# Four graph layers on one core: table blocks of five instead of six, a multiplication moved to GpSimd, and a reordered last pair pass

## What is computed

```python
def _L1_gnn_ref(z, P, W1, b1, W2, b2, Wu, bu):      # "maximum"
    m1z = z @ W1.T + b1
    m2z = z @ W2.T + b2
    pair = relu(m1z[:, :, None, :] + m2z[:, None, :, :])
    mask = (swapaxes(P, 1, 2) != 0)[..., None]
    m = max(where(mask, pair, -inf), axis=2)
    return relu(concatenate((z, m), axis=-1) @ Wu.T + bu)

def _L2_gnn_ref(input, adj, W, a_w, a_b):           # "heads", H = 8
    h = input @ W
    ...
    att = softmax(where(adj[:, None] > 0, e, NEG_INF), axis=-1)
    return einsum('bhij,bjf->bif', att, h) / att.shape[1]

def _L3_gnn_ref(x, A_init, ...):                    # "pairs"
    D = abs(x[:, :, None, :] - x[:, None, :, :])
    h = D @ W1.T + b1            # statistics over all pairs of all graphs
    h = leaky((h - m) / sqrt(v + EPS) * g1 + be1)
    s = where(A_init > 0, h @ W2.T + b2, NEG)
    y = softmax(s) @ x @ Wg.T + bg   # statistics over all nodes of all graphs
    y = leaky((y - mg) / sqrt(vg + EPS) * gg + beg)
    return concatenate([x, y], axis=2) @ Wt.T + bt
```

## Time and profile before

| | us |
|---|---|
| median of 3 runs (2192.54 to 2194.11) | 2193.01 |
| the profiled execution | 2195.21 |
| its span, first to last instruction | 2193.4 |

### The profile page before, as it was taken

How to read it: one execution, slowest core, us unless ns; L and a number is a source line. 1 busy time by engine, 2 the same in 40 slices (tenths; PEclk the granted TensorE clock), 3 DMA queues, 4 the chain that set the end, 5 groups by cost and what they waited for, 6 DMA issues and landing times. The chain is left out here.

```text
span 2193.4 us, 43678 instructions
## 1 busy us (share of the span) xinstructions
PE 1839.7 (84%) x13419; PEld 1195.8 (55%) x13419; DVE 1829.3 (83%) x2792; ACT 1459.0 (67%) x3325; POOL 471.6 (22%) x346
## 2 busy tenths in 40 slices
PE   2978988888885888886799999999999577778786
PEld 1857777776772656565655555555555133333346
DVE  5988788888885999997799999999999466767666
ACT  0544444444443888885278888888888577777773
POOL 1510000000001111101444444444444100000001
PEclk9989999999996999997599999999999799999998
DMA  6000000000000000000045555555555889999972
GB/s 173 0 7 2 1 0 0 0 0 0 0 1 12 6 5 4 5 6 20 1 201 222 220 220 220 228 222 220 220 220 227 311 331 349 355 349 355 353 279 77
DMA packets 122544, 297.31 MB, mean 136 GB/s; under 512 B 20352, under 2 KB 56456, under 8 KB 122264
## 3 DMA queue, kind: packets, MB, share of 16 engines
q1 hardware_dynamic: 105336, 287.69, 35.0%
q10 hardware_dynamic: 16896, 8.39, 1.3%
q0 software_dynamic: 256, 0.56, 0.1%
HBM read 154.78 MB, written 141.82 MB: 135 GB/s over the span
## 5 line engine op out<-in xcount | busy, mean ns | idle before, releaser
L1234 POOL TENSOR_TENSOR v_pairs<-hd 128x2048 f32 (+1 forms) x64 | 269.4, 4209 | 310.8 <-DVE v_pairs L1259 310.8
L1319 ACT ACTIVATE v_hid<-v_psW 128x1024 f32<-128x1024 f32 x256 | 263.3, 1028 | 85.9 <-PE v_psW L1357 85.9
L1255 DVE TENSOR_TENSOR v_pairs<-v_psX,hd 128x2048 f32<-128x2048 f32 x128 | 292.3, 2287 | 17.5 <-PE v_psW L1357 17.5
L1357 PE MATMUL v_psW<-v_pairs,p_w1T 128*64 128x512 f32 x1024 | 288.8, 597 | 0.0
L724 DVE TENSOR_REDUCE m_part<-m_psS 128x128 f32<-128x1024 f32 (+1 forms) x192 | 216.9, 1130 | 68.6 <-PE m_psS L603 68.4
L1322 ACT ACTIVATE v_junk<-v_psW 128x1024 bf16<-128x1024 f32 x256 | 263.1, 1028 | 0.0
L1357 PE MATMUL v_psW<-v_pairs,l_w1T 128*64 128x512 f32 (+1 forms) x1024 | 252.5, 587 | 0.0
L603 PE MATMUL m_psS<-m_onehot,m_tableT 64*128 64x128 f32 x2816 | 217.3, 293 | 34.2 <-DVE m_part L724 18.0
L1348 PE MATMUL v_psW<-p_ends,v_weights 128*64 128x512 bf16 x1536 | 235.3, 381 | 4.3 <-DMA v_fold<-in_c_fold_dram 4.3
L956 ACT ACTIVATE a_ex<-a_eu,a_nmx 128x128 f32<-128x128 f32 x512 | 197.8, 389 | 37.3 <-PE a_psA L925 28.7
L603 PEld LDWEIGHTS m_psS<-m_onehot,m_tableT 64*128 64x128 f32 x2816 | 180.6, 194 | 59.3 <-ACT m_tableT L666 19.4
(11 more groups left out here) (253 smaller groups left out, 3539.6 us busy)
## 6 DMA issues: line engine op xcount, KB each, us to landing
pair_hidden<-v_hid SPq DMA_DIRECT2D x256, 512.0 KB, 2.6
s_h<-pair_hidden SPq DMA_DIRECT2D x128, 1024.0 KB, 7.3
s_wide<-pair_scores SPq DMA_DIRECT2D x64, 128.0 KB, 6.0
adj_ring<-in_adj_dram ACTq DMA_DIRECT2D x16, 256.0 KB, 6.2
x_all<-in_x_dram ACTq DMA_DIRECT2D x16, 256.0 KB, 6.0
out_dram<-o_res SPq DMA_DIRECT2D x16, 256.0 KB, 2.3
pair_scores<-s_rot SPq DMA_DIRECT2D x64, 32.0 KB, 6.0
p_ends<-in_c_ends_dram SPq DMA_DIRECT2D x1, 1024.0 KB, 4.8
```

The lines of the kernel that those rows point to most:

```text
L1234: nc.gpsimd.tensor_tensor(D[:, home(u, SLABS - 1), :].rearrange("c (h d i) -> c h d i", h=2, i=N), one, far, ALU.subtract).then_inc(psub_d ...
L1255: nc.vector.tensor_tensor(slab(s), own, windows(hd, n, s)[1], ALU.max).then_inc(max_done, 1)
L1319: nc.scalar.activation(hid[:, s, :], psW[:, buf, :], ACT.Identity, accum_out=hsum[:, bass.ds(m, 1)]).then_inc(evacuated, 1)
L1357: last = nc.tensor.matmul(psW[half * HID:half * HID + HID, buf, c:c + w], product[:, :], D[:, home(u, s), half * HALF + c:half * HALF + c ...
```

## The change

- **Blocks of five.** `BLK = 5`, `NBLK = 28`, `SUB = 32`, `NCH = 7` chunks of four blocks, `NG = 2` items of 4 and 3 chunks, `ITEMS = 8` a quad. Five table steps; the last one covers 16 blocks. `select` uses products of 32 rows; `q` runs over four and each `q` has a bank of `psS`, so that an item fills all four banks and waits for the reduction of the item before. `reduce` reads four banks; `merge` is one maximum of two tiles.
- **Order of the maximum.** PE and ACT prepare two items ahead (`select` first, `prepare(at + 2)` last in a slot). The update's bias and its `hT` half are done early (`own`, slot 5), the `mT` half in slot 2 of the next quad. The sum with the own term goes to a tile `both`, the bias instruction on DVE is gone. `prepare` of the table starts after DVE's first fill (`padded`).
- **Heads.** The multiplication with the reciprocal sums is done by POOL; `ex`, `zs` and `rz` have four buffers instead of two. POOL's normalization of quad g+2 follows in slot 1.
- **Pass 2.** The slabs of pass 1 and the load slots are one tile (`ring`); SP issues the first four loads at the end of pass 1. The read-back is two DMAs of 64 rows of 512 B; the first half lands in `fwd` itself, and two copies of 64x64 replace the addition. The features' part of the output product is done in pass 2 (`xo_mm`), where POOL adds the output bias to `x` and DVE adds the product.
- **Output.** Four products a quad instead of eight, one addition on DVE instead of two, no copy on POOL; the output DMA reads `k.x`.

```diff
-BLK = 6
-NBLK = (N + BLK - 1) // BLK
+BLK = 5
+NBLK = 28
-NCH = NBLK // 2
+NCH = NBLK // 4
...
-                    pe.wait_ge(reduced, done(n - 2))
-                    for c in range(4 * r, min(4 * r + 4, NCH)):
-                        for q in (0, 1):
+                    pe.wait_ge(reduced, done(n - 1))
+                    for c in chunks(r):
+                        for q in range(4):
                             rows = slice(SUB * q, SUB * q + SUB)
-                            last = nc.tensor.matmul(psS[:, 2 * par + q, b(c % 4)], tableT[rows, par, c % 4, :],
+                            last = nc.tensor.matmul(psS[:, q, b(c % 4)], tableT[rows, par, c % 4, :],
                                                     onehot[rows, par, c % 4, :], start=True, stop=True)
...
+                def own(g, p):
+                    pe.wait_ge(added, done(g - 1))
+                    nc.tensor.matmul(psU[:, :].rearrange("n (b c) -> n b c", c=C), one[:, :],
+                                     k.bu[0:1, :].unsqueeze(1).broadcast_to([1, G, C]), start=True, stop=False)
+                    for i in range(G):
+                        last = nc.tensor.matmul(psU[:, b(i)], hT[:, p, b(i)], k.wuT[:, 0, :], start=False, stop=False)
+                    last.then_inc(own_mm, 1)
...
                     for at in range(ITEMS):
...
+                        select(g, *divmod(at, NG))
+                        if at == 0 and next:
+                            turn(g + 1, 1 - p)
+                        if at == 1 and next:
+                            second(g + 1, 1 - p)
+                        if at == 2 and prev:
+                            update(g - 1, 1 - p)
+                        if at == 3 and next:
+                            first(g + 1, 1 - p)
+                        if at == 5:
+                            own(g, p)
+                        if at + 2 < ITEMS:
+                            prepare(g, *divmod(at + 2, NG))
...
-                    nc.vector.tensor_reduce(mx[:, b(i)], part[:, i, :, :].rearrange("z r i -> z i r"), AX.X,
-                                            ALU.max).then_inc(merged, 1)
+                    nc.vector.tensor_tensor(mx[:, b(i)], part[:, i % 2, 0, :], part[:, i % 2, 1, :], ALU.max).then_inc(merged, 1)
...
                     for at in range(ITEMS):
                         reduce(g, at)
                         if at == 0:
                             if prev:
                                 add_own(g - 1, 1 - p)
+                            tables(g, p, 2, LATE)
                         if at == 1:
+                            merge(g, 0)
+                            tables(g, p, 3, EARLY)
+                        if at == 2:
+                            tables(g, p, 3, LATE)
+                        if at == 3:
+                            merge(g, 1)
+                            if next:
+                                tables(g + 1, 1 - p, 0, EARLY)
+                        if at == 4:
+                            if prev:
+                                update(g - 1)
+                            if next:
+                                tables(g + 1, 1 - p, 0, LATE)
+                        if at == 5:
+                            merge(g, 2)
+                            if next:
+                                tables(g + 1, 1 - p, 1, EARLY)
+                            if prev:
+                                statistics(g - 1)
...
+                def slot(g, p, i, behind, ahead):
+                    n = g * G + i
+                    if behind(3):
+                        at = (i - 3) % G
+                        pool.wait_ge(recip, done(n - 3))
+                        per_head = ex[:, at, :].rearrange("n (h j) -> n h j", j=N)
+                        nc.gpsimd.tensor_tensor(per_head, per_head, rz[:, at, :].unsqueeze(2).broadcast_to([N, HEADS, N]),
+                                                ALU.mult).then_inc(scaled, 1)
+                    if i == 1 and ahead(2):
+                        normal(g + 2, p)
...
+                sp.wait_ge(w_mm, done(B * SLABS - 1))
+                for s in range(SLABS):
+                    sp.wait_ge(stored[s], 16 * B)
+                for j in range(4):
+                    load_products(sp, D, loaded, hidden, j)
...
                     sp.wait_ge(written[m % 2], 16 * (m // 2 + 1))
+                    sp.wait_ge(m_mm, done(m - 2))
+                    src = scratch[m % 4].rearrange("(i j) -> i j", j=2 * N)
+                    sp.dma_start(fwd[0:HID, m % 2, :], src[0:HID, 0:N]).then_inc(back[m % 2], 16)
                     sp.wait_ge(fwd_ready, done(m - 2))
-                    sp.dma_start(wide[:, m % 2, :], scratch[m % 4].rearrange("(i j) -> i j", j=2 * N)).then_inc(back[m % 2], 16)
...
+                    sp.dma_start(wide[HID:N, m % 2, :], src[HID:N, HID:HID + N]).then_inc(back[m % 2], 16)
...
-                        nc.vector.tensor_tensor(fwd[:, p, :], wide[:, p, 0:N], wide[:, p, N:2 * N], ALU.add).then_inc(fwd_ready, 1)
+                        nc.vector.tensor_copy(fwd[HID:N, p, 0:HID], wide[HID:N, p, HID:N])
+                        nc.vector.tensor_copy(fwd[HID:N, p, HID:N], wide[HID:N, p, 0:HID]).then_inc(fwd_ready, 1)
+                    if five:
+                        m = n - 5
+                        dve.wait_ge(xo_mm, done(m))
+                        dve.wait_ge(xb_ready, done(m))
+                        xs = k.x[:, bass.ds(m * C, C)]
+                        nc.vector.tensor_tensor(xs, psO[:, 0:C], xs, ALU.add).then_inc(x_added, 1)
...
                         pe.wait_ge(hg_ready, done(m - 1))
+                        pe.wait_ge(x_added, done(m - 1))
                         pe.wait_ge(hx_ready, done(m))
                         nc.tensor.matmul(psG[:, 0:C], hx[:, q, :], k.wgT[:, :], start=True, stop=True).then_inc(hg_mm, 1)
+                        nc.tensor.matmul(psO[:, 0:C], hx[:, q, :], k.wtT[:, 0, :], start=True, stop=True).then_inc(xo_mm, 1)
...
                     for i in range(G):
-                        nc.tensor.matmul(psU[:, p, b(i)], hq[:, p, b(i)], k.wtT[:, 0, :], start=True, stop=False)
-                        last = nc.tensor.matmul(psU[:, p, b(i)], yn[:, p, b(i)], k.wtT[:, 1, :], start=False, stop=True)
+                        last = nc.tensor.matmul(psU[:, p, b(i)], yn[:, p, b(i)], k.wtT[:, 1, :], start=True, stop=True)
```

More of the change, by code:

```diff
@@ L688, in _ @@
                 first(0, 0)
+                item(0, 0)
                 quads(act, quad)
@@ L757, in quad @@
                 def quad(g, p, prev, next):
-                    def ahead(i, steps):
-                        if next:
-                            tables(g + 1, 1 - p, i, steps)
                     for at in range(ITEMS):
                         reduce(g, at)
-                        if at % NG == NG - 1:
-                            merge(g, at // NG)
                         if at == 0:
@@ L1059, in phase_pairs @@
         hidden = nc.dram_tensor("pair_hidden", (B * SLABS, N, HALF), F32).ap()
+        ring = k.sb(ctx, "pair_ring", [N, SLABS + 1, SC], F32)
+        loaded = [k.sem(f"s_loaded{i}") for i in range(4)]
         with ExitStack() as hctx:
@@ L1685, in _ @@
             def _(dve):
-                for s in (leaky, biased, res_ready):
+                for s in (leaky, summed):
                     dve.sem_inc(s, BIAS)
```

249 lines of the change are left out of this document (107 added, 142 removed).

## The result

The changed kernel takes 2130.9 us (median of 4 runs, 2129.6 to 2132.9), the kernel before 2193.6 in the same comparison: a ratio of 0.9712, 95% interval 0.9695 to 0.9728. The profiled execution has a span of 2131.1 against 2193.4. So 63 us were gained where I had forecast 113; the sign was right, the size and the range were not.

The account below looks back on a forecast made before the run. Bounds: no full engine in the maximum, DVE in heads, a ring of ACT and PE in pass 2. Gains 63 (maximum) + 36 (heads) + 2 + 0 + 12 (output) = 113 from 2195.2: 2082.2, by the median 2080; range 2055 to 2122.

Parts of the forecast that it names:

- the picking's price: Maximum: rounds of four records on 32 rows; 32 records take 1.16 us and 24 take 0.94.
- C: Maximum: products on 32 rows run one after the other, 0.11 us a record; stage 190 longer, kernel 2333, chance 4%.
- the 2220 of the prediction: Maximum: if the skill's 81 ns a product held for the new products, slots of 2.7 and 2.1, kernel some 2220.
- I add 0.6 for clock dips and imperfect order: Maximum: 0.6 us added to a quad of 27.2, giving 27.8 against 31.86, a gain of 61 us.
- rival A: Maximum: PE becomes its bound, by record price or a clock staying at 1.2 GHz; no gain there, 2141, chance 12%.
- everything behind that wait on PE ... comes while DVE reduces, at most 2 us against 1.75 or more: Maximum: PE's turn, projections, own and prepare, at most 2 us, run during DVE's reduction of 1.75 us or more.
- the tail: End of the maximum: a gain of 2 us, as half the products and the bias are out of the way.
- rival B: Heads: DVE stays the bound because it and GpSimd block each other; 2109 us, chance 14%.
- Heads: the term: Heads: ACT bounds next, 4.6 us a graph instead of 5.18, a gain of 36 us for 63 graphs.
- Pass 2, the start and the output: Gains of 0 in pass 2, 2 us from pass 1 to pass 2, and 12 us in the output.
- D: Whole kernel: everything at its floor, gains of 72 + 43 + 5 + 15, 2058 us, chance 7%.
- E: Pass 2: a new wait, the `x` addition or read-back on the ring, 0.3 us a graph, 2100 us, chance 8%.

Follow-up runs that it names:

- m_all: Changed kernel with own part in three pieces, match products done four times, GpSimd's normalization held back until item 1 is picked: 2092.0 us, ratio 0.9534.
- h_att: Changed kernel with DVE's copy of the heads' attention moved from before its leaky part to after it: ratio 0.9628, 18 us less than the changed kernel.
- m_fill: Changed kernel with every match product of the maximum done four times over: ratio 0.9651, 13 us less than the changed kernel.

## Why the prediction was wrong

**Maximum, the picking's price: right.** 1.17 and 0.95 us for 1.16 and 0.94. The rival that they are dearer (C) is dead at 0.028 a record.

One sum beside it doesn't come out: with slots of 2.7 and 2.1 the time is about 2195, and the 2220 of the prediction follows only with 0.2 for two hand-overs added to each. Nothing rested on it.

**Maximum, "I add 0.6 for clock dips and imperfect order": the step that failed.** The mechanism stood in the text, that a PE with waits in every slot is granted a lower clock (rival A), and the term for its mild form was mis-sized. It measured 1.8 a quad against the forecast's slots: 1.0 in slot 5, where in ten of 14 inner quads the own part and the preparation ran slowed and the gap was 3.3 instead of 1.8, and 0.8 in slot 7, where in eleven of 14 the picking did (up to 2.09 us for 1.17). The mean clock hardly showed it, 0.90 instead of 0.94; the slow stretches lay on products that DVE waits for. The sum should have had a term for them, since the prediction itself counted about one dip a quad, showed what it costs, and the picking had just been put on the path in every slot. One picking of 32 records at 1.2 GHz is 0.9 us.

**Maximum, "everything behind that wait on PE ... comes while DVE reduces, at most 2 us against 1.75 or more": right at 2.4 GHz only.** In slot 5 PE is ready 2.33 us after its picking at full clock, 0.40 after the reduction's end, and DVE's other work hides this. At 1.2 GHz it is 3.2 to 3.9 us, and nothing hides it. I had seen that the two numbers hardly fit (2 against 1.75), and didn't ask what they are at the lower clock.

**Maximum, the tail: wrong sign.** I gave it a gain of 2, which the last update has (6.6 to 4.6 us), and did not look at the last quad. It lost 7.7. Of these 2.1 stay when the clock is up (25.1 in m_all against 23.0 before: the reductions are 2.5 longer), and 5.6 went with the clock of 0.72, while PE was busy 21 of 31 us. The forecast's form "a quad times 15, and 2" left the sixteenth quad out.

**Maximum, what GpSimd does beside DVE: not seen.** I looked at this blocking for the heads, where it did nothing: the multiplication lasts 1.90 and DVE's split instructions are as before (733, 743 and 684 ns). But no split instruction in the trace ran beside a multiplication, so rival B's blocking was not put to the test there; it didn't come about. What did run beside it, the leaky part and the maximum, kept its length (1213 and 1220 ns). The blocking came in the maximum, where the sum and the table steps have both inputs in SBUF: 0.5 in slot 0., from which my table steps of 1.50 a graph came, couldn't show it: in the kernel before no table step was longer than others of its shape (at most 13 ns), as the normalization ran beside reductions. The new order brought it beside the steps.

**Heads: the term was mis-sized, and the sentence that sized it was wrong.** "What is queued behind it on PE, the next scores, has over 3 us until ACT wants it": ACT waited for just these (10.4 us between 700 and 960), and DVE's leaky part was behind the same products by a second way, its own instruction for the attention, which I had not listed among what waits; h_att shows that this was most of it. 4.6 was ACT's busy time and a little more; with the chain reciprocal, GpSimd, PE in the ring it was 4.8, and 4.5 when the ring was opened. Rival B's size (29 us less gain) was too large and its cause was another.

**Pass 2, the start and the output: right within 3 us.** The period stayed (ACT's first instruction at 1881.34, 1887.74 and 1894.26, 6.4 to 6.5, as in the earlier trace rows); the product added on PE found its gap, and PE's wait for ACT was 1.1 to 1.2 after 1.30, as I had written:

```profile
1881.34 1.24 ACT L1619 ACTIVATE s_hid<-pair_ring,p_beta,p_alpha 128x1024 f32<-128x1024 f32 x1 [0.82 <-PE s_psR L1664]
...
1891.85 0.49 PE L1697 MATMUL s_psA<-s_dg,s_ex 128*128 128x128 f32 x2 [1.17 <-ACT hy L1632]
```

The output takes 1.48 a quad, two quads in 2.97 against 4.64 in the earlier trace rows:

```profile
2107.06 0.69 DVE L1766 TENSOR_TENSOR x_all<-o_psU,x_all 128x512 f32 x1
...
2110.03 0.69 DVE L1766 TENSOR_TENSOR x_all<-o_psU,x_all 128x512 f32 x1
```

**The range.** It reached from the floor (D) to rivals B and E, each taken alone. Two terms failed at once, by 35 and by 11 to 18, and no case had both. The terms shared an assumption, that what stands on PE between two uses is hidden: in the maximum it failed at the lower clock, in the heads by the order of the instructions.

## What to carry to other kernels

When a buffer becomes single and a producer moves onto the path, write out that producer's whole queue slot by slot, with the sum of all that stands in one slot, and work it out at the slower clock as well: what was hidden at 2.4 GHz was on the path at 1.2. A mean can hide two kinds of rounds (here gaps of 1.8 and 3.3); list the rounds one by one, since those that went well show what the others lost, without another run. Where a wait is placed at the head of an engine's slot, ask what of the ring stands behind it, and put the instruction nobody hurries for behind the one the ring needs. Edits of one slot can need each other: alone they hardly changed slot 5 or made it worse, and the three together took 0.93 off.

## What the runs showed of the hardware

Products on 32 rows run four at a time with their own weight loads: 32 records of 128 columns in 1.17 us, 64 in 2.07, so 0.112 us a round of four at 2.4 GHz, and 2.09 us for 32 at 1.2 GHz, 0.213 a round.

Useless work made the kernel faster: 1247 more matmul records in 380 us raised the granted clock from 0.89 to 0.97 and m_fill took 13 us off the whole.

GpSimd multiplied 1024 elements with a broadcast operand in 1.90 us, where DVE had needed 1.23, and beside it DVE's leaky part (1213 ns) and maximum (1220), with one input in SBUF each, were no longer than alone. Beside GpSimd's normalization, DVE instructions with both inputs in SBUF were: two table steps 1.69 us instead of 0.84, a sum of 512 elements up to 1.29 instead of 0.68, a merge 0.70 instead of 0.29.
